# A graph network's setup: edge counts by source tile on ACT, and the fills of the message rows in the middle rounds only

## The chip, the cores and the metric

The kernel runs on one core of one Trainium2 chip. The metric is the device time of one execution in microseconds (us). It is given as the median of several runs; beside them stands one execution under the hardware profiler, from which all rows below come. The engines are PE (matrix products), DVE (vector), ACT (activations), POOL (general, and it issues the indirect DMAs) and SP (issues direct DMAs).

## The reference

Four layers of a graph network over 6250 nodes of 128 features and 100000 edges, sorted by destination. Each layer gathers rows of the nodes by `src`, weighs or transforms them, and sums them by `dst`:

```
edge_index = jnp.stack([src, dst])
h = relu(layernorm(x));  x = x + L0(h, edge_index, edge_weight, ...)
h = relu(layernorm(x));  x = x + L1(h, edge_index, ...)            # attention, two layers
h = relu(layernorm(x));  x = x + L2(h, edge_index, edge_attr_64)   # messages through an MLP
h = relu(layernorm(x));  x = x + L3(h, edge_index, ...)            # attention, 8 heads
# in L0: the message of an edge is h[col] * fsum, with fsum from tanh and cos of its edge_weight;
# row = edge_index[0] = src, col = edge_index[1] = dst, and it is summed by row
```

## The kernel before

Nodes lie in 49 tiles of 128 rows (`NB2` = 50 with one to make it even). Edges lie as 128 partitions x 784 columns (`EP`, `EC`). The kernel has a setup and then six stages, each closed by `stage_of_work` (L99 to L106): the stage's semaphores are cleared and all engines meet.

The setup sorts edges into slots: 832 tiles of 128 slots (`NT`, `SLOTS`), in which each tile holds edges of one node tile. There is one such order by destination (q = 0) and one by source (q = 1). `key[q]` holds each edge's node tile number. The setup goes so:

- **Counts** (`count_round`, L588 to L599, DVE). For each of 50 tiles and each q one instruction compares all 784 columns with the tile's number and sums the hits into `count[q]`. `looped` runs it in 25 rounds of two tiles. The compare's elementwise result goes to `equal`, scratch that shares its memory with `slots`. Then `counts_ready` is set; PE turns the counts into offsets (L468 to L471).
- **Small work** (L601 to L613): `slots` is cleared, the filter's scale and bias are made, and `filt_ready` is set. ACT's filter loop begins there (L512 to L521, Tanh, with PE's products at L462), ending in a Sin (L523).
- **Chunk 0** of the slot search (`slot_round`, DVE with help of POOL, L424 to L428), then L691 to L697, which need the filter loop, then `slot_rows`, which sets `chunk_ready`. Six more chunks follow on DVE alone.
- **Scatter** (L434 to L449, POOL). 28 rounds (`scatter_rounds` = EC / (2 * SC), SC = 14) of two halves h; each half is 14 indirect DMAs (one a column) that write 128 edge records to `rec_d`, 782 in all. Before a half, SP loads its edge attributes (L366, or L362 and L363) once the scatters of the same half one round before have landed (`scattered[h]`), and ACT copies the rest of the record (L545, L547). POOL waits for both. Ahead of them, it waits for `filled`: SP's DMA at L341 that writes empty records to the whole of `rec_d`. The last thing that POOL does in the setup is to wait for all scatters.
- **Fills of message rows** (`pad_messages`, SP, L349 to L352). Layer 0 later scatters its messages to `msg_d`, and its unused rows must hold an empty message. `msg_d` has 104 units (`NT // G`). `part` = 104 // 28 = 3 and `left` = 20. `body(i)` writes `part` units ahead of round i for i from 1 to 27; behind the rounds come units 0 to 2 and the 20 left over. SP then waits for all (`msgs_padded`).
- DVE ends its setup with the first layer norm (L199, L211), while the scatters run.

Behind the setup comes the destination pass of layer 0 (`layer0_dst_pass`, block at L1127, its scatters at L1279, first DMA L1147, DVE's first L1192), and the layers after it. SP's queue carries direct DMAs in the order written; POOL's indirect DMAs have a queue of their own.

Of the kernel before, what the change touches and what calls it, by code (L numbers as in the profile page):

```python
# [21 lines left out]
ALU = mybir.AluOpType  # L22
# [16 lines left out]
EP, EC = 128, 784  # L39
# [52 lines left out]
def gnn(nc, a, out):  # L92
# [3 lines left out]
    def sem(name):  # L96
        names[0] += 1
        return nc.alloc_semaphore(name=f"{name}_{names[0]}")
# [22 lines left out]
    with ctx:  # L121
# [92 lines left out]
        def setup():  # L214
# [33 lines left out]
            eqs, cums = [tb([EP, 2, CH], BF16) for h in range(2)], [tb([EP, 2, CH]) for h in range(2)]  # L248
            wt, cosine = tb([EP, EC]), tb([EP, EC])
            th = [tb([EP, EC]) for h in range(2)]  # L250
            diag = [tb([P, P]) for h in range(2)]
            tri, ones = tb([P, P]), tb([P, P])
            iota_t = tb([64, NTP])
# [24 lines left out]
            with stage_of_work():  # L278
# [10 lines left out]
                def spilled(v):  # L289
# [4 lines left out]
                    sem("steps_v"), sem("steps_p"))  # L294
                loop_a, loop_b, loop_c, counts_ready, offs_in_psum = (
                    sem(n) for n in ("loop_a", "loop_b", "loop_c", "counts_ready", "offs_in_psum"))
                filt_ready, cos_ready, upto_ready, upto_turned, reached_ready, tiles_counted = (
                    sem(n) for n in ("filt_ready", "cos_ready", "upto_ready", "upto_turned", "reached_ready", "tiles_counted"))
                tanh_ready, tanh_used = ([sem(f"{n}{h}") for h in range(2)] for n in ("tanh_ready", "tanh_used"))
# [5 lines left out]
                with nc.Block() as block:  # L305
                    @block.sync
                    def _(sp):
                        for q, v in enumerate(("dst", "src")):
                            sp.dma_start(node[q][:, 0:WHOLE], by_edge(a[v])).then_inc(nodes_in, 16)
                        sp.dma_start(wt[:, 0:WHOLE], by_edge(a["edge_weight"])).then_inc(edges_in, 16)  # L310
                        sp.wait_ge(spill_set, 3)
                        for q, v in enumerate(("dst", "src")):
                            sp.dma_start(node[q][0:SPILL, WHOLE:WHOLE + 1], spilled(a[v])).then_inc(nodes_in, 16)
                        sp.dma_start(wt[0:SPILL, WHOLE:WHOLE + 1], spilled(a["edge_weight"])).then_inc(edges_in, 16)
                        sp.dma_start(wf1, a["L0_gnn_Wf1"].to_broadcast([P, NF])).then_inc(edges_in, 16)
                        sp.dma_start(bf1, a["L0_gnn_bf1"].unsqueeze(0).to_broadcast([P, NF])).then_inc(edges_in, 16)
                        sp.dma_start(bf2, a["L0_gnn_bf2"].unsqueeze(0).to_broadcast([P, NF])).then_inc(edges_in, 16)
                        sp.dma_start(wf2, a["L0_gnn_Wf2"].unsqueeze(0).to_broadcast([P, NF, NF])).then_inc(edges_in, 16)
                        for t, v in vec.values():
                            sp.dma_start(t[:, :], v.unsqueeze(0).to_broadcast([P, D])).then_inc(weights_in, 16)  # L320
                        for l, t in enumerate(bias_row):
                            sp.dma_start(t[:, 0:D], a["L1_gnn_bias"][l, :].unsqueeze(0).to_broadcast([P, D])) \
                                .then_inc(weights_in, 16)
                        for t, v in mat.values():
                            sp.dma_start(t[:, :], v).then_inc(weights_in, 16)
                        for l in range(3):
                            sp.dma_start(wx[l][:, 0:D], a["L1_gnn_W"][l] if l < 2 else a["L3_gnn_W"]).then_inc(weights_in, 16)
                            for q, v in enumerate(("att_src", "att_dst")):
                                v = a["L1_gnn_" + v][l, :] if l < 2 else a["L3_gnn_" + v].rearrange("h c -> (h c)")
                                sp.dma_start(att_col[l][q][:, :], v.rearrange("(p a) -> p a", a=1)).then_inc(weights_in, 16)  # L330
                        for t, v in ((bi1_col, a["L0_gnn_bi1"]), (bu1_col, a["L2_gnn_bu1"]), (gs_col, a["L2_gnn_global_state"])):
                            sp.dma_start(t[:, :], v.rearrange("(p a) -> p a", a=1)).then_inc(weights_in, 16)
                        for t, v in ((wm1, "L2_gnn_Wm1"), (wm2, "L2_gnn_Wm2"), (wu1, "L2_gnn_Wu1"), (wu2, "L2_gnn_Wu2")):
                            sp.dma_start(t[:, :], a[v]).then_inc(weights_in, 16)

                        sp.wait_ge(x_zero, 1)
                        sp.dma_start(X[:, 0:FULL, :], a["x"][0:FULL * P, :].rearrange("(b p) f -> p b f", p=P)).then_inc(x_in, 16)
                        sp.dma_start(X[0:REST, FULL, :], a["x"][FULL * P:N, :]).then_inc(x_in, 16)

                        sp.wait_ge(pads, 1)  # L340
                        sp.dma_start(rec_d.rearrange("(k p j) w -> p k (j w)", p=P, j=G),  # L341
                                     pad_rec[:, :].unsqueeze(1).to_broadcast([P, NT // G, G * RW])).then_inc(filled, 16)


                        msg_v = msg_d.rearrange("(k p j) w -> p k (j w)", p=P, j=G)
                        scatter_rounds = EC // (2 * SC)
                        part = NT // G // scatter_rounds
                        left = NT // G - part * scatter_rounds

                        def pad_messages(k, n):  # L350
                            sp.dma_start(msg_v[:, bass.ds(k, n), :],
                                         pad_msg.unsqueeze(1).to_broadcast([P, n, G * MW])).then_inc(msgs_padded, 16)  # L352

                        def body(i, first):
                            if not first:
                                pad_messages(i * part, part)
                            for h in range(2):
                                if not first:
                                    sp.wait_ge(scattered[h], i * (16 * SC))
                                if h and isinstance(i, int) and i:  # L360
                                    at = WHOLE - (EC - SC)
                                    sp.dma_start(rec[h][:, 0:at, 0:EA], attr_v[:, EC - SC:WHOLE, :]).then_inc(attr_in[h], 16)  # L362
                                    sp.dma_start(rec[h][0:SPILL, at, 0:EA],  # L363
                                                 a["edge_attr_64"][EP * WHOLE:E]).then_inc(attr_in[h], 16)
                                else:
                                    sp.dma_start(rec[h][:, :, 0:EA],  # L366
                                                 attr_v[:, bass.ds((2 * i + h) * SC, SC), :]).then_inc(attr_in[h], 16)
                        body(0, True)
                        with sp.Fori(1, scatter_rounds - 1) as i:
                            body(i, False)  # L370
                        body(scatter_rounds - 1, False)
                        pad_messages(0, part)
                        if left:
                            pad_messages(scatter_rounds * part, left)
                        sp.wait_ge(msgs_padded, 16 * (scatter_rounds + (1 if left else 0)))

                    @block.gpsimd
                    def _(pool):
# [129 lines left out]
                    @block.scalar  # L508
                    def _(act):
                        st = Steps(act, steps_a)  # L510
                        act.wait_ge(filt_ready, 1)
                        def body(i, first):  # L512
                            for h in range(2):
# [56 lines left out]
                    def _(dve):  # L570
# [10 lines left out]
                        for q in range(2):  # L581
                            st.then(v.tensor_single_scalar(row[q][:, :], node[q][:, :], 7, ALU.logical_shift_right))
                            st.then(v.tensor_copy(key[q][:, :], row[q][:, :]))
                            st.then(v.tensor_single_scalar(row[q][:, :], node[q][:, :], P - 1, ALU.bitwise_and))
                            st.then(v.tensor_copy(meta[:, :, 4 * q:4 * q + 1], row[q][:, :].unsqueeze(2)))
                        st.then(v.tensor_copy(meta[:, :, 1:2], node[1].unsqueeze(2)))


                        def count_round(i, first):
                            for h in range(2):  # L590
                                for q in range(2):
                                    if not first:

                                        dve.wait_ge(loop_a, i * 4 + 2 * h + q - 3)
                                    b = i * 2 + h
                                    v.tensor_scalar(equal[2 * h + q], key[q], iota_row[0:EP, bass.ds(b, 1)], 0.0,
                                                    ALU.is_equal, ALU.add, accum_out=count[q][:, bass.ds(b, 1)]).then_inc(loop_a, 1)
                        looped(dve, NB2 // 2, count_round)
                        dve.wait_ge(loop_a, NB2 * 2)  # L599
                        dve.sem_inc(counts_ready, 1)  # L600
                        st.then(v.memset(slots, 0.0))  # L601
                        st.then(v.memset(slots[:, 0, WHOLE + 1:EC], float(SKIP)))
# [1307 lines left out]
```

## Time and profile before

| | us |
|---|---|
| median of 3 runs | 7402.07 (7401.49 to 7413.68) |
| the profiled execution, its own time | 7404.54 |
| its span, first to last instruction | 7402.5 |
| setup, within the span | 0 to 1304.1 |

Over the span PE is busy 3331.8 us (45%), DVE 3299.0 (45%), ACT 1691.6 (23%), POOL 5000.4 (68%). These shares are means over stages with different limits, so the prediction goes by stretches of the setup. In a row, a start is in us from the span's start, and L596 is line 596 of the kernel. A tile name such as XI, Y, H or ACC is the memory in which the setup has carved its scratch, not what the layers keep there.

### The profile page before, as it was taken

The page shows a single profiled execution, that of the slowest core. Times are in us where ns is not written, and L with a number is a line of the kernel's source. Part 1 is how long each engine was busy: PE and PEld are TensorE (multiplying, and loading weights), DVE is VectorE, ACT ScalarE, POOL GpSimd, SP SyncE. Part 2 cuts the span into 40 slices and gives each one's busy share as a digit, 9 for nine tenths or more (in the row PEclk, how much of TensorE's full clock was granted, in tenths as well). Part 3 has the DMA queues.
Part 4 walks back from the last instruction along what each step waited for, and adds up shares of the span by engine and source line. Part 5 has one row for each costly group of instructions (what it writes and reads, how often), then busy time and mean ns, then how long its engine had stood idle before and what let it go on. Part 6 is the DMA issues. An engine that isn't in the chain of part 4 may idle for free. (4 is left out here: it accounts for less than half of the span.)

```text
span 7402.5 us, 89274 instructions
## 1 busy us (share of the span) xinstructions
PE 3331.8 (45%) x17325; PEld 2957.3 (40%) x17326; DVE 3299.0 (45%) x10231; ACT 1691.6 (23%) x4176; POOL 5000.4 (68%) x5176
## 2 busy tenths in 40 slices
PE   2200000444443864444434444445777775444443
PEld 1100000444443753444434444434777664344443
DVE  8777732333323663333344333335333336544445
ACT  2200000211111963222223222223222224000000
POOL 1677777677777726777755777764777770777775
PEclk9655555666666986555556555566666677666666
DMA  6122234444443624444434444433444440444443
GB/s 225 57 92 91 96 97 151 153 156 156 155 154 133 218 79 136 129 134 131 133 91 129 133 133 130 133 100 107 134 135 134 134 128 30 132 132 133 132 132 105
DMA packets 507505, 942.53 MB, mean 127 GB/s; under 512 B 204347, under 2 KB 240683, under 8 KB 507304
## 3 DMA queue, kind: packets, MB, share of 16 engines
q1 hardware_dynamic: 349288, 637.41, 25.9%
q0 software_dynamic: 158144, 304.31, 15.8%
q8 instruction: 26, 0.43, 0.0%
q14 instruction: 47, 0.39, 0.0%
HBM read 673.90 MB, written 270.84 MB: 128 GB/s over the span
## 5 line engine op out<-in xcount | busy, mean ns | idle before, releaser
L1371 POOL DMA_INDIRECT edge_buf<-node_table,ixr x1664 | 1571.6, 944 | 619.4 <-issue 507.9
L1371 POOL DMA_INDIRECT Y<-node_table,ixr x1664 | 1569.7, 943 | 521.1 <-issue 519.9
L1111 DVE TENSOR_TENSOR ACC<-ACC,bank 128x129 f32 (+2 forms) x3744 | 1092.9, 292 | 1102.2 <-PE bank L1098 469.2
L1279 POOL DMA_INDIRECT layer_messages<-edge_buf,ixr x832 | 809.3, 973 | 295.7 <-issue 263.0
L1538 PE MATMUL bank<-adc,turned_buf 128*128 x2496 | 340.3, 195 | 1476.1 <-issue 571.7
L440 POOL DMA_INDIRECT edge_records<-edge_buf x782 | 791.2, 1012 | 255.1 <-issue 246.2
L1538 PEld LDWEIGHTS bank<-adc,turned_buf 128*128 128x128 bf16 x2496 | 257.0, 103 | 1606.7 <-issue 1552.4
L1098 PE MATMUL bank<-edge_buf,Y 128*128 128x129 f32 (+2 forms) x3744 | 821.1, 406 | 142.7 <-ACT edge_buf L1524 96.5
L1098 PE MATMUL bank<-Y 128*128 128x129 f32 (+1 forms) x3328 | 763.1, 420 | 158.6 <-ACT Y L1524 88.7
L1098 PEld LDWEIGHTS bank<-edge_buf,Y 128*128 128x128 f32 x3744 | 764.0, 309 | 173.1 <-DVE ACC L1111 136.7
L1098 PEld LDWEIGHTS bank<-Y 128*128 128x128 f32 x3328 | 713.4, 323 | 181.5 <-issue 89.0
L1486 DVE TENSOR_REDUCE pk<-bank 128x16 f32<-128x48 f32 (+1 forms) x312 | 100.5, 322 | 999.6 <-DMA Y<-node_table,ixr 501.3
L1227 PE MATMUL bank<-ident,Y 128*128 128x128 f32 x832 | 204.3, 427 | 738.7 <-DVE Y L1064 736.5
L1227 PEld LDWEIGHTS bank<-ident,Y 128*128 128x128 f32 x832 | 163.2, 223 | 761.5 <-issue 568.1
L1657 PE MATMUL bank<-wmbT,turned_buf 64*128 64x128 f32 x1664 | 293.0, 345 | 192.3 <-DVE Y L1596 101.3
L1657 PEld LDWEIGHTS bank<-wmbT,turned_buf 64*128 64x128 f32 x1664 | 266.7, 248 | 224.6 <-issue 210.1
L489 PE MATMUL bank<-Y,H 128*128 128x2 f32 (+1 forms) x6 | 1.4, 359 | 775.2 <-DVEq L717 775.2
L1239 PE MATMUL bank<-H,Y 128*128 x1664 | 318.9, 373 | 2.5 <-DVEq L1189 2.5
L1239 PEld LDWEIGHTS bank<-H,Y 128*128 128x128 f32 x1664 | 318.5, 293 | 2.8 <-issue 2.8
L1267 ACT COPY Y<-bank 128x512 f32<-128x512 f32 x208 | 123.8, 595 | 840.3 <-PE bank L1239 840.1
L1177 DVE COPY edge_buf<-XI 128x8 f32 (+1 forms) x104 | 18.7, 180 | 664.6 <-DMA layer_messages<-edge_buf,ixr 664.6
L489 PEld LDWEIGHTS bank<-Y,H 128*128 128x128 f32 x6 | 1.4, 326 | 775.4 <-issue 775.4
(279 smaller groups left out, 5319.1 us busy)
## 6 DMA issues: line engine op xcount, KB each, us to landing
Y<-onehots SPq DMA_DIRECT2D x416, 512.0 KB, 3.6
turned_buf<-onehots_turned SPq DMA_DIRECT2D x312, 256.0 KB, 3.8
edge_buf<-edge_records SPq DMA_DIRECT2D x208, 288.0 KB, 2.9
onehots<-Y SPq DMA_DIRECT2D x104, 512.0 KB, 2.7
layer_messages<-ACC SPq DMA_DIRECT2D x28, 1584.0 KB
XI<-layer_messages SPq DMA_DIRECT2D x78, 528.0 KB, 3.7
edge_records<-H SPq DMA_DIRECT2D x1, 29952.0 KB
onehots_turned<-turned_buf SPq DMA_DIRECT2D x104, 256.0 KB
```

Of the source, the lines that this page charges most:

```text
L440: pool.indirect_dma_start(rec_d, bass.IndirectOffsetOnAxis(ap=ixs[h][:, j:j + 1], axis=0), rec[h][:, j, :], None, bounds_check=SLOTS - 1, ...
L1098: ins = nc.tensor.matmul(places.at(q, j, w), tiles_of_half(onehots)[:, j, :], messages[:, j, 0:w], start=True, stop=True)
L1111: nc.vector.tensor_tensor(acc, acc, places.at(q, j, w), ALU.add).then_inc(added, 1)
L1177: nc.vector.tensor_copy(rows[h][:, :, D:D + 1], fields[:, bass.ds(t, G), R_SLOC - EA:R_SLOC - EA + 1]) \
L1227: ins = nc.tensor.transpose(bank[j // 4][:, (j % 4) * P:(j % 4) * P + P], tiles_of_half(oh[h])[:, j, :], ident[:, :])
L1239: ins = nc.tensor.matmul(bank[2 + j // 4][:, (j % 4) * P:(j % 4) * P + P], ohT[h][:, j * P:j * P + P], Hflat[:, bass.ds(at[j] * AW, D)], s ...
L1267: nc.scalar.copy(ohT[h][:, at], bank[n][:, :]).then_inc(ohT_ready, 1)
L1279: pool.indirect_dma_start(msg_d, bass.IndirectOffsetOnAxis(ap=ixr[h][:, j:j + 1], axis=0), rows[h][:, j, 0:MW], None, bounds_check=SLOTS - ...
L1371: pool.indirect_dma_start(ring[q][:, j, 0:w], None, table, bass.IndirectOffsetOnAxis(ap=ixr[q][:, j:j + 1], axis=0)).then_inc(rows_in[q], 16)
L1486: st.then(nc.vector.tensor_reduce(ps, picks(q).rearrange("p (j t k) -> p j k t", j=G, t=3), AX.X, ALU.add))
L1538: ins = nc.tensor.matmul(picks(q)[:, j * 6 * heads:(j + 1) * 6 * heads], ohbT[q][:, j * P:j * P + P], adc[:, bass.ds(at[j] * (6 * heads), ...
L1657: ins = nc.tensor.matmul(bank[2 + j // 4][:, (j % 4) * P:(j % 4) * P + P], attrT[q % 2][:, j * P:j * P + P], wmbT[:, :], start=True, stop= ...
```

## The change

ACT gets a loop of 50 Sign activations ahead of its filter loop: sign(b + 0.5 - key) over the source keys, summed along the columns into `signs[b + 1]`. The sum is (edges with key at most b) less (edges with a greater key), so the difference of neighbouring sums is twice the count of tile b. DVE counts by destination only, then waits for all the signs, subtracts and halves. SP's fills are 26 of 4 units, ahead of rounds 1 to 26, and none behind the rounds.

```diff
+            sign_at, signs = tb([EP, NB2]), tb([EP, NB2 + 1])
@@ SP
-                        part = NT // G // scatter_rounds
-                        left = NT // G - part * scatter_rounds
+                        part = -(-(NT // G) // (scatter_rounds - 2))
+                        assert part * (scatter_rounds - 2) == NT // G
...
                         def body(i, first):
-                            if not first:
-                                pad_messages(i * part, part)
+                            if not isinstance(i, int):
+                                pad_messages(i * part - part, part)
...
                         body(scatter_rounds - 1, False)
-                        pad_messages(0, part)
-                        if left:
-                            pad_messages(scatter_rounds * part, left)
-                        sp.wait_ge(msgs_padded, 16 * (scatter_rounds + (1 if left else 0)))
+                        sp.wait_ge(msgs_padded, 16 * (scatter_rounds - 2))
@@ ACT
                         st = Steps(act, steps_a)
+                        act.wait_ge(src_keys, 1)
+
+                        def sign_round(i, first):
+                            for h in range(2):
+                                b = i * 2 + h
+                                if not first:
+                                    act.wait_ge(sign_sums, i * 2 + h - 1)
+                                nc.scalar.activation(equal[2 * h + 1], key[1], ACT.Sign, scale=-1.0,
+                                                     bias=sign_at[:, bass.ds(b, 1)],
+                                                     accum_out=signs[:, bass.ds(b + 1, 1)]).then_inc(sign_sums, 1)
+                        looped(act, NB2 // 2, sign_round)
                         act.wait_ge(filt_ready, 1)
@@ DVE
                             st.then(v.tensor_copy(meta[:, :, 4 * q:4 * q + 1], row[q][:, :].unsqueeze(2)))
+                            if q:
+                                st.then(v.tensor_scalar(sign_at, iota_row[0:EP, 0:NB2], 0.5, None, ALU.add))
+                                st.then(v.memset(signs[:, 0:1], -float(EC)))
+                                dve.sem_inc(src_keys, 1)
                         st.then(v.tensor_copy(meta[:, :, 1:2], node[1].unsqueeze(2)))
...
                         def count_round(i, first):
                             for h in range(2):
-                                for q in range(2):
-                                    if not first:
-
-                                        dve.wait_ge(loop_a, i * 4 + 2 * h + q - 3)
-                                    b = i * 2 + h
-                                    v.tensor_scalar(equal[2 * h + q], key[q], iota_row[0:EP, bass.ds(b, 1)], 0.0,
-                                                    ALU.is_equal, ALU.add, accum_out=count[q][:, bass.ds(b, 1)]).then_inc(loop_a, 1)
+                                if not first:
+
+                                    dve.wait_ge(loop_a, i * 2 + h - 1)
+                                b = i * 2 + h
+                                v.tensor_scalar(equal[2 * h], key[0], iota_row[0:EP, bass.ds(b, 1)], 0.0,
+                                                ALU.is_equal, ALU.add, accum_out=count[0][:, bass.ds(b, 1)]).then_inc(loop_a, 1)
                         looped(dve, NB2 // 2, count_round)
-                        dve.wait_ge(loop_a, NB2 * 2)
+                        dve.wait_ge(loop_a, NB2)
+
+
+                        dve.wait_ge(sign_sums, NB2)
+                        st.then(v.tensor_tensor(count[1], signs[:, 1:NB2 + 1], signs[:, 0:NB2], ALU.subtract))
+                        st.then(v.tensor_scalar(count[1], count[1], 0.5, None, ALU.mult))
                         dve.sem_inc(counts_ready, 1)
```

## Rows read from the trace of the kernel before

**Rows 1.** Windows view: stretch, length, busy us of PE, PEld, DVE, ACT, POOL, clock, DMA share, GB/s.

```profile
250.50:1288.20 1037.70, 8.84 (x20) 3.10 (x20) 622.30 (x2014) 21.43 (x114) 791.20 (x782) 0.50 0.31 102
1304.10:7402.50 6098.40, 3220.57 (x17030) 2906.55 (x17030) 2459.11 (x7659) 1577.59 (x3915) 4150.80 (x4267) 0.66 0.43 130
```

**Rows 2.** Groups of instructions on DVE, setup: busy us, mean ns, idle before.

```profile
L596 DVE TENSOR_SCALAR_CACHE_REDUCE XI<-Y,iota_row 128x784 bf16<-128x784 bf16 x100 | 95.1, 1024 | 0.0
```

**Rows 3.** Timeline, counts and the work behind: start, us, engine, line, [idle before].

```profile
19.81 6.29 DVE L585 CAST ACC<-ACC 128x784 f32<-128x784 int32 x1
...
27.04 1.03 DVE L596 TENSOR_SCALAR_CACHE_REDUCE XI<-Y,iota_row 128x784 bf16<-128x784 bf16 x1
...
122.05 0.08 DVE L596 DVE_READ_ACCUMULATOR XI<-Y,iota_row  x1
...
122.64 1.36 DVE L601 MEMSET XI<- 128x1568 f32 x1 [0.51 <-DVE XI L596]
```

**Rows 4.** ACT in the setup: timeline at the filter loop, and a short copy.

```profile
130.39 0.40 ACT L517 ACTIVATE XI<-ident,H 128x128 f32<-128x128 f32 x1 [128.30 <-DVEq L614]
...
130.69 1.03 ACT L519 ACTIVATE XI<-XI,H 128x784 f32<-128x784 f32 x1
...
131.63 0.39 ACT L517 ACTIVATE XI<-ident,H 128x128 f32<-128x128 f32 x1
...
231.72 1.28 ACT L523 ACT_TABLE_LOAD   x1
...
233.01 0.95 ACT L523 ACTIVATE XI<-XI,Y 128x784 f32<-128x784 f32 x1
...
249.25 0.20 ACT L547 COPY edge_buf<-ACC 128x14 int32<-128x14 int32 x1
```

**Rows 5.** Timeline, end of chunk 0, first scatter.

```profile
241.96 0.57 DVE L691 TENSOR_SCALAR XI<-XI 128x784 f32<-128x784 f32 x1 [0.40 <-POOL XI L428]
...
250.52 1.30 POOL L440 DMA_INDIRECT edge_records<-edge_buf  x1 [8.59 <-issue]
```

**Rows 6.** The scatters: landing times (from the line's own view), and timeline beside a fill.

```profile
DMA to landing us min/median/max: 2.2/2.2/6.8
...
1221.29 0.59 SPq L351 DMA_DIRECT2D layer_messages<-ACC  x1
1222.13 0.97 POOL L440 DMA_INDIRECT edge_records<-edge_buf  x1 [0.30 <-issue]
...
1287.22 0.97 POOL L440 DMA_INDIRECT edge_records<-edge_buf  x1 [0.30 <-issue]
```

**Rows 7.** The closing: timeline, then SP's queue waits (us in total, times, longest).

```profile
1257.43 0.95 SPq L351 DMA_DIRECT2D layer_messages<-ACC  x2
...
1304.10 0.84 SPq L1147 DMA_DIRECT2D edge_buf<-edge_records  x2
...
SPq L305 <- DMA layer_messages<-ACC: 36.5, 1, 36.5
```

**Rows 8.** Block ends by line (duration ns, start us), and the pass compared with.

```profile
L305 POOLq DRAIN  x1: 9054/9054/9054, 1294.1 to 1294.1; - x1
...
L1127 POOLq DRAIN  x1: 3985/3985/3985, 2394.5 to 2394.5; - x1
...
2392.16 0.97 POOL L1279 DMA_INDIRECT layer_messages<-edge_buf,ixr  x1 [0.30 <-issue]
```

**Rows 9.** Timeline of SP's queue behind the fill of the record table.

```profile
39.46 79.09 SPq L366 DMA_DIRECT2D edge_buf<-in_edge_attr_dram  x2
```

**Rows 10.** Scatters' time to landing from 1285 to 1305, and windows of the closing.

```profile
edge_records<-edge_buf POOLq DMA_INDIRECT x3, 6.7
...
1265.00:1270.00 5.00, 0.00 (x0) 0.00 (x0) 0.00 (x0) 0.00 (x0) 3.78 (x5) 0.50 1.02 380
```

**Rows 11.** PE's filter products, and windows at their end.

```profile
L462 PE MATMUL bank<-XI 128*128 128x392 f32 x256 | 99.1, 525 | 10.0 <-ACT XI L519 8.8
...
230.00:235.00 5.00, 4.19 (x17) 2.29 (x16) 4.39 (x15) 4.45 (x8) 1.72 (x4) 1.00 0.00 0
```

More of the change, by code:

```diff
@@ L296, in setup @@
                     sem(n) for n in ("loop_a", "loop_b", "loop_c", "counts_ready", "offs_in_psum"))
+                src_keys, sign_sums = sem("src_keys"), sem("sign_sums")
                 filt_ready, cos_ready, upto_ready, upto_turned, reached_ready, tiles_counted = (
```

## The prediction

> **What bounds the kernel now.** I read the windows view first, cut at the setup's own events [rows 1]. The span is 7402.5 us. The setup takes the first 1304.1 us of it, and the change touches only that. The layers behind it (6098.4 us) keep their code, so whatever the setup loses or gains moves them as a block.
>
> Next I read the timeline of the setup, to see which engine holds it at each moment.
>
> First DVE counts. It runs 100 compare-and-sum instructions [rows 2], the first at 27.04 us; the last one's sum is read at 122.05 [rows 3]. They fill 95.1 us, so they start 0.95 us apart. Nobody else works: ACT is idle for 128.3 us until DVE has set the filter's inputs [rows 4], and PE has no counts to work on.
>
> Then comes chunk 0 of the slot search on DVE, which ends with L691 at 241.96 and the rows behind it; POOL issues its first record scatter at 250.52 [rows 5].
>
> From there POOL is the bound: 782 scatters in 1037.7 us, 1.33 us each [rows 1, 6]. DVE is busy for 622.3 us of them and ACT for 21.4, so neither sets that pace. The last scatter is issued at 1287.22 [rows 6].
>
> Last comes the end of the setup, 16.9 us from that scatter to the next stage's first DMA at 1304.10 [rows 7]. SP waits 36.5 us there for the last fills of the message rows, 3 and 20 units, which it issued only at 1257.43 [rows 7]. That wait is over at 1294.9 (1257.43 + 0.95 + 36.5), and is not what is late: POOL, behind its own wait for the scatters, spends 9.05 us in a DRAIN from 1294.1 to 1303.2 [rows 8]. All engines leave the block behind it.
>
> So three stretches in series matter: the counts, the scatters, the closing.
>
> **Part 1, the counts.** DVE loses 50 of 100 counting instructions, 50 x 0.95 = 47.5 us. It gains four small ones: before its loop an add on 128x50 and a memset (about 0.2 + 0.1 us), behind it a subtract and a multiply on 128x50 (about 0.25 us each with its wait: an estimate between the 0.08 of the sum's read [rows 3] and the 0.57 of 784 columns in L691 [rows 5]). DVE's own loop would then run from 27.35 to 27.35 + 47.5 + 0.1 = 74.95.
>
> ACT gets 50 Sign activations on 128x784 with a sum. No such operation stands in the trace, so I bound it. The same size with two pointer operands (Tanh) takes 1.03 us, with one (Sin, as Sign has) 0.95 [rows 4]. They overlap: a Tanh starts at 130.69 and the instruction behind it at 131.63 [rows 4], 0.94 us apart, so 0.09 is hidden. A Sign alone would step by 0.95 - 0.09 = 0.86 us. Its sum must be read, as DVE does in a record of its own (0.08 us [rows 3]); a short copy on ACT takes 0.20 whole [rows 4], 0.11 with the same overlap. I take the middle, 0.16, for the read: 1.02 us a Sign. ACT starts when src_keys is set, at about 26.5 (behind L585's cast at 26.10, before L586), so it ends at 26.5 + 50 x 1.02 = 77.5; with DVE's two small instructions and the signal, counts_ready falls at 78.1 in place of 122.1. **Part 1 gives 44.0 us.** Bounds: if the read costs nothing, DVE is last, 75.5, gain 46.6; if nothing overlaps (0.95 + 0.20 = 1.15 us), 84.6, gain 37.5. The value taken is nearest to the Tanh row (0.94 apart), which is the same engine, size and kind of loop.
>
> The waits added: ACT waits for the sign before the last one, which is always done when the last one starts; DVE waits for all 50 signs before it clears the slots that hold ACT's scratch output. Behind that wait stand DVE's whole setup, PE's count products and ACT's own filter loop; so it is the point where the two engines meet, and ACT is 2.5 us the later one. A second table load, should Sign need another set than Tanh, is 1.28 us [rows 4] and falls into the 8.3 us between the end of the counts and ACT's first filter step (122.05 to 130.39 [rows 3, 4]): nothing.
>
> The Trainium skill ("ScalarE: Activation LUTs", What ACT_TABLE_LOAD costs) prices an ACTIVATE with one pointer at 280 ns + 0.833 ns an element, 933 ns here, and says that neighbours overlap by 93 ns. By that a Sign steps by an estimated 0.84 us and DVE, not ACT, would be last unless the read costs over 0.13 us; the trace's 0.95 us agrees within 2%. The page gives no price for the read of the sum.
>
> Does the whole rest move up by 44 us? What else could hold POOL's first scatter: the fill of the record table lands by about 118, since SP's next issue is stuck behind it for 79.09 us from 39.46 [rows 9]. POOL would want it at about 206, so 88 us of cover are left; without the cover that fill would set the start. The first attribute loads sit behind the same fill. The filter loop (ACT and PE, until 233.96) ends 8.0 us before DVE's L691 asks for it at 241.96 [rows 4, 5], and moves by the same amount. From there all is paced by POOL's issue.
>
> **Part 2, the fills of the message rows.** Before: 27 fills of 3 units beside the rounds, and two at the end, 3 and 20 units. After: 26 of 4 units in rounds 1 to 26, none at the end. A unit is 528 KB (128 partitions x 8 x 132 words). In the rounds this adds a third to each fill, 2.1 MB. At the 380 GB/s of the closing [rows 10] that is 5.6 us in a round of two halves of 14 x (0.97 + 0.30) = 17.8 us, issued ahead of SP's wait for the scatters. The attribute load issued behind it goes out a half later. The scatters don't slow: with a fill issued at 1221.29 the next starts at 1222.13, and its 0.97 us are those of 1287.22 [rows 6]. So nothing is charged, with 12 us of cover in each half.
>
> At the end, the last scatters landed in 6.7 us beside the fills, where 2.2 is the median [rows 10, 6]. POOL's DRAIN began 6.9 us behind the last issue. A block whose POOL also ends in scatters but with idle DMA engines is the destination pass: last scatter 2392.16, DRAIN 3.985 us from 2394.5 to 2398.5 [rows 8], so 6.3 us from last issue to the end. With the 0.9 us from the DRAIN's end to the next stage, the setup would close 7.2 us behind its last scatter in place of 16.9. **Part 2 gives 9.7 us.** Bounds: if the DRAIN keeps its 9.05 us and only the landing gets shorter, 1287.2 + 2.3 + 9.05 + 0.9 = 1299.5, gain 4.6; if there were none at all, 1290.4, gain 13.7. I take the destination pass, which is the same kind of work.
>
> The Trainium skill ("DMA: Bandwidth & Descriptors", Queues, rings and completion order) says that an engine goes round robin between the queues that have work, a whole packet at a time; by that a scatter beside a fill waits for fill packets on each engine, which is what 6.7 against 2.2 us shows. It says nothing of the DRAIN.
>
> **Sum.** 44.0 + 9.7 = 53.7 us off the profiled span, 7402.5, giving 7348.8. The profiled execution's own time is 7404.5, 2.0 above its span, and the median of the runs is 7402.07, 2.5 below it; I take the gain off the median: **7348.4 us.** With the bounds of both parts the gain runs from 42.1 to 60.3, so 7341.8 to 7360.
>
> **Rivals.**
> (a) *The DRAIN stays.* SP's fills had all landed at 1294.9 and it still ran for 8.3 us more, so it may be a cost of this block; against it, the destination pass, with 832 scatters by its code, has 3.985. Gain 44.0 + 4.6: 7353.5.
> (b) *The sum makes ACT serial.* If each Sign must leave the engine and be read before the next is dispatched, and each hand-over costs what DVE idles between its last count and L601, 0.51 us [rows 3], a Sign takes 0.95 + 0.20 + 0.51 = 1.66 us: 26.5 + 83 + 0.6 = 110.1, gain 12.0 + 9.7: 7380.4. For it: no ACT sum is in the trace; against it: DVE does the same with no gap.
> (c) *Simple work is slow on ACT.* The whole gain is gone once the signs end at 131.2, a step of 2.09 us. At three times DVE's 0.95 us a Sign takes 2.85: 26.5 + 142.5 + 0.6 = 169.6, 47.5 us later than 122.1, less 9.7: 7440, slower. The Trainium skill ("ScalarE: Activation LUTs", Rules for kernel authors) advises VectorE for such operations, up to about 3 times faster in bf16. By that rule this rival would hold; the trace speaks against it, 0.94 us on ACT beside 0.95 on DVE.
> (d) *The filter loop falls to the low clock.* PE's 256 matmuls there are busy 99.1 us at a granted clock of 1.00 (2.4 GHz) [rows 11]. DVE gives them 110 us. At 0.50 (1.2 GHz) they would take 198, 88 more than that: 7348 + 88 = 7436, slower than before. It eats the whole gain once the mean clock in the loop is under 99.1 / (110 + 53.7) = 0.61. Against it: PE was idle before this loop too, longer than it will be, and had 1.00 until 235 [rows 11]; the 0.50 stands in the stretch where PE is busy for 8.84 us of 1037.7 [rows 1].
> (e) *The earlier counts don't reach POOL*, because a transfer or another engine holds the first scatter; only part 2 is left, 7392, within 0.2%. The 88 us of cover speak against it.
>
> **Chances.** Forecast 0.69, (a) 0.20, (b) 0.06, (c) 0.01, (d) 0.02, (e) 0.02. A measurement of this kernel tells 0.2% (15 us) from no change. Faster by more: forecast, (a) and (b), 0.95; same 0.02; slower 0.03. The range takes in the bounds of both parts and (a), and a few us of spread between runs: 7341 to 7362; (b) to (e), 0.11, stay outside.
>
> **What would show it.** Right: 50 Sign activations on ACT about 1.0 us apart ending near 77.5 while DVE counts until 75; the first scatter near 206.5; 782 scatters in 1038 us as before; the last one near 1243; no fill behind the rounds; POOL's closing DRAIN near 4 us; next stage at 1250.4. Wrong: Sign steps over 1.15 us; a DRAIN still near 9 us; a scatter pace over 1.33 us because of the larger fills; a stretch from counts to first scatter longer than 128.4 us.

## The result, and the profile after

The changed kernel takes 7349.3 us (median, 7346.76 to 7352.97); the kernel before took 7401.78 beside it (7401.48 to 7413.68). The ratio is 0.9928, with a 95% interval of 0.9915 to 0.9942: 52.5 us faster, where 53.7 had been forecast. The sum came so close in part by luck: two of its terms are off in opposite directions.

| stretch of the setup, us | before | forecast | after |
|---|---|---|---|
| to the first record scatter | 250.52 | 206.5 | 203.76 |
| first to last scatter issued | 1036.7 | 1036.7 | 1036.16 |
| last scatter to next stage | 16.9 | 7.2 | 12.47 |
| setup | 1304.1 | 1250.4 | 1252.39 |
| span less setup | 6098.4 | 6098.4 | 6095.1 |

In the rows, a q behind an engine's name is the engine's own instruction queue. First the groups on ACT and DVE of the changed kernel, in the setup (busy us, mean ns, idle before):

```profile
L517 ACT ACTIVATE XI<-Y 128x784 bf16<-128x784 bf16 x50 | 46.6, 932 | 24.3 <-DVEq L599 24.3
L517 ACT ACTIVATION_READ_ACCUMULATOR XI<-Y x48 | 8.9, 185 | 0.0
...
L517 ACT ACT_TABLE_LOAD x1 | 1.3, 1283 | 0.8 <-PEq L1916 0.8
L533 ACT ACT_TABLE_LOAD x1 | 1.3, 1283 | 0.0
...
L609 DVE TENSOR_SCALAR_CACHE_REDUCE XI<-Y,iota_row 128x784 bf16<-128x784 bf16 x50 | 47.6, 1026 | 0.0
```

[rows 2] had 100 counts on DVE; now it has 50, at the same pace. The timeline of the two loops' start and end:

```profile
26.34 0.95 ACT L517 ACTIVATE XI<-Y 128x784 bf16<-128x784 bf16 x1 [24.26 <-DVEq L599]
...
27.20 0.19 ACT L517 ACTIVATION_READ_ACCUMULATOR XI<-Y 128x1 f32 x1
27.29 0.93 ACT L517 ACTIVATE XI<-Y 128x784 bf16<-128x784 bf16 x1
27.32 1.03 DVE L609 TENSOR_SCALAR_CACHE_REDUCE XI<-Y,iota_row 128x784 bf16<-128x784 bf16 x1
...
72.83 0.18 ACT L517 ACTIVATION_READ_ACCUMULATOR XI<-Y  x1
...
74.82 0.08 DVE L609 DVE_READ_ACCUMULATOR XI<-Y,iota_row  x1
74.94 0.21 DVE L616 TENSOR_TENSOR XI<-XI 128x50 f32<-128x50 f32 x1
75.19 0.19 DVE L617 TENSOR_SCALAR XI<-XI 128x50 f32<-128x50 f32 x1
...
75.58 0.64 PE L468 MATMUL bank<-XI 128*128 128x50 f32 x2 [75.58 <-DVEq L618]
```

ACT is done at 73.01 and DVE at 74.90. So ACT is the early one, and DVE never waits: its subtraction follows its own last count. In [rows 3] the last sum was read at 122.05, 47.2 us later. PE's count products, which begin at 75.58, began at 122.34 before.

The groups above have two table loads, one ahead of the first Sign and one ahead of the Sin. So none stands between the Signs and the Tanhs. The timeline of the filter loop's end, as in [rows 4]:

```profile
184.42 1.28 ACT L533 ACT_TABLE_LOAD   x1
185.72 0.95 ACT L533 ACTIVATE XI<-XI,Y 128x784 f32<-128x784 f32 x1
```

The timeline of the scatters (first and last), which answers to [rows 5, 6], and of the next stage's first DMA, which answers to [rows 7]:

```profile
203.76 1.30 POOL L439 DMA_INDIRECT edge_records<-edge_buf  x1 [8.59 <-issue]
...
1239.92 0.97 POOL L439 DMA_INDIRECT edge_records<-edge_buf  x1 [0.30 <-issue]
...
1252.39 1.14 SPq L1165 DMA_DIRECT2D edge_buf<-edge_records  x2
```

And the end of the setup's block by line (duration in ns, start in us), which answers to [rows 8]. Each engine's part of a block ends with a DRAIN:

```profile
L307 SPq COMPARE_BRANCH  x1: 38/38/38, 1210.1 to 1210.1; - x1
L307 POOLq COMPARE_BRANCH  x1: 38/38/38, 1242.2 to 1242.2; - x1
L307 POOLq DRAIN  x1: 9054/9054/9054, 1242.3 to 1242.3; - x1
```

SP leaves at 1210.1, long before it is needed; POOL passes its wait 2.3 us behind the last scatter, where it had been 6.7. But the DRAIN lasts 9.054 us, as before, where 3.985 had been forecast. That is the forecast's miss.

The two profiled spans differ by 55.0 us (7402.5 and 7347.5), of which 51.7 lie in the setup and 3.3 in the layers, whose code the change leaves alone. Over the twelve profiled kernels of this case that ran at the pace of the one before, span less setup lies between 6093.5 and 6100.7 us, with no order in it; so I count these 3.3 us as spread, and the setup's 51.7 us as the effect. The medians, 52.5 us apart, agree with that within their spread.

### The profile page after: what moved, and what is told of

Same layout as the page of the kernel before. It is cut to its first block and busy times, and to the rows that moved or that the text cites. A ratio compares the mean times of both kernels' runs of the same rounds, so it can differ in the third digit from the quotient of the medians.

```text
span 7347.5 us, 89302 instructions
## 1 busy us (share of the span) xinstructions
PE 3339.2 (45%) x17325; PEld 2965.8 (40%) x17326; DVE 3231.2 (44%) x10135; ACT 1737.8 (24%) x4276; POOL 4999.3 (68%) x5176
```

## The experiments

All but the second start from the changed kernel. Stretches are read from each run's trace.

**The counts alone** (the changed kernel with SP's fills as before):

```diff
-                        part = -(-(NT // G) // (scatter_rounds - 2))
-                        assert part * (scatter_rounds - 2) == NT // G
+                        part = NT // G // scatter_rounds
+                        left = NT // G - part * scatter_rounds
...
+                        pad_messages(0, part)
+                        if left:
+                            pad_messages(scatter_rounds * part, left)
...
```

> The counts of the change with the fills of before (27 of 3 units beside the rounds, 3 and 20 units at the end). In the trace of the changed kernel the first scatter came 46.8 us earlier and the closing was 4.4 us shorter. Theory, the two parts add: first scatter at 203.8, the closing 16.9 us from the last scatter to the next stage as before, time 7401.8 - 46.8 = 7355. Rival, the parts meet (the wider fills slow the scatters or the earlier counts move them into the record table's fill): the scatters' stretch is not 1036 us and the time is off 7355 by more than 4.

Measured 7355.3 us beside 7402.75 (ratio 0.9938, 0.9922 to 0.9955), 47.45 less. First scatter at 204.62, scatters' stretch 1036.5, closing 16.9. With the 4.25 of the next run the parts add to 51.7 us, for 52.5 together. The first scatter comes 0.86 us later than the changed kernel's: DVE's cast ahead of the counts (L595 in the changed kernel) already starts 0.84 us later (20.45 for 19.61), so a single trace gives part 1 to some 0.9 us.

**The fills alone** (the kernel before with the changed kernel's SP code):

> The fills of the change with the counts of before. Theory (the DRAIN stays at its 9.05 us, only the landing of the last scatters gets shorter): first scatter at 250.5, closing 12.4 us in place of 16.9, time 7401.8 - 4.4 = 7397.4. Rival as in the prediction's main line (the DRAIN shrinks to 4 us without the fills beside it): closing 7.2 us, time 7392.

Measured 7398.5 us beside 7402.75 (ratio 0.9995, 0.9985 to 1.0004): too small to tell from no change by the time alone. In its trace the first scatter is at 250.25, the last at 1286.93, and the next stage starts at 1299.39: a closing of 12.5 us. Its DRAIN:

```profile
L305 POOLq DRAIN  x1: 9054/9054/9054, 1289.3 to 1289.3; - x1
```

So the second part is worth 4.4 us of closing: without fills at the end the last scatters land sooner (the DRAIN starts 2.4 us behind the last of them, 6.9 before). The larger fills cost the scatters nothing: 1036.7 us from first to last, as before.

**Each Sign twice**, which makes ACT late on purpose:

```diff
...
+                                if not first:
+                                    act.wait_ge(twice, i * 2 + h - 1)
+                                nc.scalar.activation(th[h], key[1], ACT.Sign, scale=-1.0,
+                                                     bias=sign_at[:, bass.ds(b, 1)],
+                                                     accum_out=spare[:, bass.ds(b, 1)]).then_inc(twice, 1)
                         looped(act, NB2 // 2, sign_round)
+                        act.wait_ge(twice, NB2)
```

> The changed kernel with each Sign activation run twice (the second into spare scratch and a spare sum), so ACT has 100 of them. It makes ACT the late engine on purpose. Theory, a Sign with its sum takes 0.93 us from start to start (the read of the sum is hidden but for 0.09): the signs end at 26.3 + 93.4 = 119.7, counts about 44.5 us later than in the changed kernel, and all behind moves one for one: first scatter near 248.3, time 7349 + 44.5 = 7394. Rival, there is slack behind the counts (something else holds the first scatter): less than 44.5. Rival of the prediction's price, 1.02 us a Sign: ends at 128.5, first scatter near 257.

Measured 7397.07 us (one execution). Timeline of its last signs, and its first scatter:

```profile
117.17 0.93 ACT L523 ACTIVATE XI<-Y 128x784 f32<-128x784 bf16 x1
118.00 0.18 ACT L523 ACTIVATION_READ_ACCUMULATOR XI<-Y  x1
118.10 0.93 ACT L518 ACTIVATE XI<-Y 128x784 bf16<-128x784 bf16 x1
118.94 0.19 ACT L518 ACTIVATION_READ_ACCUMULATOR XI<-Y  x1
...
119.87 0.18 ACT L523 ACTIVATION_READ_ACCUMULATOR XI<-Y  x1
...
248.06 1.30 POOL L440 DMA_INDIRECT edge_records<-edge_buf  x1 [8.59 <-issue]
```

The signs start 0.93 us apart (117.17, 118.10) also with 100 of them, and end at 120.05. The second Sign of each pair writes a sum that nobody uses; DVE waits only for the first. DVE's subtraction came at 119.23 for 74.94, 44.3 us later, and the first scatter too (248.06 for 203.76): the stretch behind the counts has no slack, which is what makes part 1 count in full.

**POOL's last wait on ACT:**

```diff
@@ POOL
-                        for h in range(2):
-                            pool.wait_ge(scattered[h], 16 * (SC * (last + 1) - (unused if h else 0)))
@@ ACT, behind its last rounds
+                        for h in range(2):
+                            act.wait_ge(scattered[h], 16 * (SC * (EC // (2 * SC)) - (EC - WHOLE - 1 if h else 0)))
```

> The changed kernel, with POOL's last wait (for the landing of all scatters) taken by ACT, so POOL's closing DRAIN is dispatched right behind its last scatter, as in the blocks that gather. Theory A, the DRAIN ends 5.3 us behind the end of the last indirect DMA (as in the gather blocks, where it starts early and lasts 20.1 us): the setup closes at about 1240.9 + 5.3 + 0.9 = 1247.1 in place of 1252.4, time 5.3 us less, 7344. Theory B, the DRAIN is a fixed 9.05 us of work behind the last scatter: 1240.9 + 9.05 + 0.9 = 1250.9, 1.5 us less. Theory C, the DRAIN's length belongs to the wait ahead of it and it grows by what the wait loses: no change.

Measured 7349.15 us, the same as the changed kernel's 7349.3. In the trace:

```profile
1240.44 0.97 POOL L439 DMA_INDIRECT edge_records<-edge_buf  x1 [0.30 <-issue]
...
1251.50 1.14 SPq L1165 DMA_DIRECT2D edge_buf<-edge_records  x2
...
L307 POOLq DRAIN  x1: 24354/24354/24354, 1226.1 to 1226.1; - x1
```

The DRAIN is dispatched some 12 scatters early and ends at 1250.45, 9.04 us behind the end of the last scatter (1241.41). That is theory B's number: some 9.05 us behind the last indirect DMA, whoever waits. The closing is 11.06 us in place of 12.47, 1.4 us that the time can't show.

**Work ahead of the DRAIN:**

```diff
+            idle_work = tb([P, 800])
...
                             pool.wait_ge(scattered[h], 16 * (SC * (last + 1) - (unused if h else 0)))
+                        for n in range(5):
+                            st.then(pool.memset(idle_work, 0.0))
```

> The changed kernel, POOL clears a spare tile of 128 x 800 five times (about 1 us each) between its last wait and the closing DRAIN. Theory A, the DRAIN's 9.05 us are work that goes on by itself once the scatters have landed, and POOL only waits for it: the DRAIN shrinks by what the clearing takes, about 5 us, and the setup closes at the same time, 12.5 us behind the last scatter. Theory B, the work starts with the DRAIN: it stays 9.05 us and the closing grows to 17.5 us.

Measured 7355.03 us (one execution). Beside this run and the next two the kernel before took 7407.80 us. The five clears and the DRAIN:

```profile
1242.15 4.05 POOL L453 MEMSET XI<- 128x800 f32 x5 [1.30 <-DMA edge_records<-edge_buf]
...
L308 POOLq DRAIN  x1: 9049/9049/9049, 1246.4 to 1246.4; - x1
```

It does not shrink by the 4.05 us: the closing grew to 16.6. Theory A is out, in that what the DRAIN waits for does not go on while POOL clears. Whether it begins with the DRAIN itself, as theory B has it, is settled by the last two runs.

**Halves of 7 columns** (`SC = 7`, 52 fills of 2 units) and **all rounds in POOL's loop** (784 scatters, none in straight code):

> The changed kernel with 56 rounds of two halves of 7 columns (SC = 7) in place of 28 of 14, and 52 fills of 2 units; 12 scatters stand in straight code behind POOL's loop in place of 26. Theory N, the closing DRAIN grows with the scatters of the code before it (1.88 us with none, 3.99 with 8 a half in the destination pass, 9.05 with 26 here, about 0.27 each): it becomes about 5.2 us, and the setup closes 3.9 us sooner. Theory K, it belongs to the kind of scatter or to the block: 9.05 stays. Beside that the scatters' stretch: 1036 us if a half of 8.9 us still covers the landing (2.2), ACT's copies (0.5) and SP's load (3.8), over 1040 if the 1 MB fills ahead of a load break that cover.

> The changed kernel with POOL's last round inside its loop: 28 rounds of two halves of 14, so 784 scatters (the two added columns hold no edge and are skipped by the bounds check), and no scatter in straight code behind the loop; SP loads the spilled edges ahead of the last attributes and waits for them. Theory N in its form of straight code: the DRAIN falls to about 2 us. In its form of scatters per half or per round (14 or 28): it stays between 6 and 10 us. Theory K: 9.05 us as before.

Measured 7353.11 us for the first (ratio 0.9926, 0.9910 to 0.9943, to the kernel before beside it) and 7358.47 for the second (one execution). Their DRAINs, in this order:

```profile
L307 POOLq DRAIN  x1: 9054/9054/9054, 1242.7 to 1242.7; - x1
```

```profile
L307 POOLq DRAIN  x1: 9217/9217/9217, 1245.8 to 1245.8; - x1
```

Theory N falls: 12 scatters in straight code, 26 or none, it stays near 9 us. The halves of 7 also show that the cover of a half holds at half its length: 1036.75 us from first to last scatter.

The 0.16 us more behind two more scatters led to another theory, that the DRAIN depends on the number of indirect DMAs in the block and starts again after some 113. **10, 15 and 24 more indirect DMAs** in POOL's idle time at the start test it; all their rows are skipped by the bounds check:

```diff
+            nowhere = tb([P, 1], I32)
...
                         pool.sem_inc(heads_in, 1)
+                        st.then(pool.memset(nowhere, 1 << 20))
+                        for n in range(15):
+                            pool.indirect_dma_start(tab_d[0], bass.IndirectOffsetOnAxis(ap=nowhere, axis=0),
+                                                    pad_msg[:, 0:D + 1], None, bounds_check=NBP * P - 1,
+                                                    oob_is_err=False).then_inc(early, 16)
+                        pool.wait_ge(early, 16 * 15)
```

> The changed kernel with 15 more indirect DMAs on POOL at the setup's start (rows that the bounds check skips), where POOL waits for the first slot round from about 26.5 to 89.6 us; the block then has 797 of them ahead of its closing DRAIN. The DRAIN was 9.054 us behind 782 scatters (in five kernels), 9.217 behind 784 and 3.985 behind the 832 of the destination pass. Theory R, it grows by 0.08 us for each indirect DMA and starts again after a fixed number of them; the three values agree when 782 - 832 and that number differ by 62 or 63 DMAs, which gives 113 to 114: 797 leaves 3 to 6, so the DRAIN falls to about 1.2 us, the setup closes 7.9 us sooner, time 7341 to 7342. Theory L, it grows with the scatters of the block without an end: 9.054 + 15 x 0.08 = 10.3 us. Theory K, it belongs to the block: 9.05 us. If the early DMAs slow DVE's counts beside them, the first scatter comes later than 203.8.

> As the run with 15, with 10 early indirect DMAs: 792 in the block. Theory R with a count that starts again every 113 DMAs: 1 is left, DRAIN about 0.8 to 1.9 us. Theory R with 113.8 (792 is then 109 past the sixth start): DRAIN 9.054 + 10 x 0.08 = 9.85 us. Theory K: 9.05.

> As the run with 15, with 24 early indirect DMAs: 806 in the block. Theory R (113 or 113.8): 10 to 15 past a start, DRAIN about 1.9 us. Theory L: 9.054 + 24 x 0.08 = 11.0 us. Theory K: 9.05 us.

Measured 7351.93 us for 15 (ratio 0.9930, 0.9916 to 0.9944, to 7402.69 for the kernel before), 7347.79 for 10 and 7350.17 for 24 (one execution each). The DRAIN with 15, and the other two have the same number:

```profile
L308 POOLq DRAIN  x1: 9049/9049/9049, 1242.5 to 1242.5; - x1
```

Theories R and L fall, as far as DMAs whose rows are all skipped can tell. DVE's last sum was read at 74.73 to 74.79 in all three (74.82 without them) and the first scatter came at 203.6, so indirect DMAs on POOL, with 15 of them from 28 to 47 us, cost DVE's counts beside them nothing.

**The sums of wf2 on POOL, with ACT's wait**, and **the changed kernel again** beside it:

```diff
@@ POOL, behind heads_in
+                        pool.wait_ge(edges_in, 16 * 6)
+                        for n in (32, 16, 8, 4, 2):
+                            st.then(pool.tensor_tensor(wf2[:, :, 0:n], wf2[:, :, 0:n], wf2[:, :, n:2 * n], ALU.add))
+                        st.then(pool.tensor_tensor(wf2_sum.unsqueeze(2), wf2[:, :, 0:1], wf2[:, :, 1:2], ALU.add))
+                        pool.sem_inc(wf2_added, 1)
@@ DVE
-                        st.then(v.tensor_reduce(wf2_sum, wf2, AX.X, ALU.add))
...
+                        dve.wait_ge(wf2_added, 1)
                         dve.sem_inc(filt_ready, 1)
```

> The changed kernel, with two more edits: the row sums of wf2 (one DVE instruction of 4.42 us between the counts and the filter loop) are made by POOL in six halving adds while it waits for the first slot round, and ACT in POOL's place waits for the last scatters, as in the run before with that edit. Theory, both stretches are in series with all else: first scatter at 203.8 - 4.4 = 199.3, closing 11.1 us, setup 5.8 us shorter, time about 7343.5. Rival, POOL's adds slow DVE's counts beside them (both work on the same memory in the changed kernel's first 75 us: DVE's cast took 6.29 us beside POOL's clear of 5.98): the counts end later than 74.9 and eat the gain.

> The changed kernel unchanged, on the chip of the run above, so that the two can be compared: 7349 by its earlier runs, first scatter at 203.8, setup closed at 1252.4; all theories say the same. It also shows how far the layers' 6095 us differ between executions of the same code.

These two ran on another chip, on which all three kernels are slower: 8974.95 us for the kernel before, 8904.95 for the changed one (ratio 0.9922, 0.9909 to 0.9936), 8914.04 for the one with the sums on POOL. The order of the first two is the same, with 70.0 us between them in place of 52.5; the kernel before has no trace there, so the other 17.5 us stay without a cause. What differs there is seen in the changed kernel's timeline of DVE in a chunk, and in what ACT waits for (us in total, times, longest):

```profile
806.15 0.45 DVE L665 TENSOR_TENSOR_SCAN XI<-Y,H 128x112 f32<-128x112 bf16 x1 [2.51 <-issue]
807.55 0.45 DVE L665 TENSOR_TENSOR_SCAN XI<-Y,H 128x112 f32<-128x112 bf16 x1 [0.95 <-issue]
...
ACT edge_buf L555 <- DVEq L698: 592.4, 6, 116.6
```

DVE's instructions take what they took (these scans 450 ns in the middle, 439 before), but 0.95 us and more pass between them with nothing to wait for. The register operations of DVE's own queue on the scans' line, 64 ns at most in the changed kernel's first trace, take up to 1395 ns here. DVE's chunks become the bound: ACT waits 592.4 us for them and the scatters' stretch is 1527.1 us. There the kernel with the sums on POOL had its last sum read at 74.73 (75.23 in the other trace), so POOL's adds did not slow the counts. DVE began its slot search 4.9 us earlier (82.71 for 87.65), but the first scatter came only 3.3 us earlier (200.99 for 204.29), where 4.4 were expected. The closing was 11.07 for 12.48, as expected. But its scatters took 3.2 us longer, so its setup ended only 1.55 us sooner (1742.32 for 1743.87), and the layers behind, of the same code, took 11.3 us more (7172.0 for 7160.7). I have no cause for these 11.3 us, and no run at the usual pace; so it isn't a version that beats the changed kernel.

The same two traces correct theory B. The closings are those of the usual pace (12.48 for 12.47 us with POOL's wait, 11.07 for 11.06 with ACT's), though the DRAIN itself is shorter. The changed kernel, then the one with the sums on POOL:

```profile
L307 POOLq COMPARE_BRANCH  x1: 700/700/700, 1733.8 to 1733.8; - x1
L307 POOLq DRAIN  x1: 7673/7673/7673, 1735.2 to 1735.2; - x1
```

```profile
1731.25 0.97 POOL L444 DMA_INDIRECT edge_records<-edge_buf  x1 [0.30 <-issue]
...
L307 POOLq DRAIN  x1: 7702/7702/7702, 1733.6 to 1733.6; - x1
```

Both DRAINs are dispatched some 1.4 us late, and both still end on time. The first ends at 1742.9, 9.1 us behind the branch that follows POOL's wait (9.1 to 9.4 at the usual pace). The second ends at 1741.30, 9.08 us behind the end of the last scatter (9.04 with ACT's wait at the usual pace). So the 9 us begin when POOL's last instruction or wait is over, and not with the DRAIN; its record shows what is left of them. Between POOL's last work and the DRAIN's end lie 9.0 to 9.4 us in all the setups traced, while the DRAIN's own record runs from 7.67 to 24.35.

## Why the prediction was right or wrong

- **DVE's loop**: forecast 27.35 to 74.95, measured 27.32 to 74.90. Right.
- **The price of a Sign**: 1.02 us was taken, 0.93 measured. The term that was mis-sized is the read of the sum. It takes 0.185 us whole, close to the 0.20 that was borrowed from a short copy, but only 0.09 of it shows in the step: the next Sign starts halfway through it (27.20, 27.29). The Sign itself adds 0.84 to the step, where 0.86 was taken. Half of the read was to be hidden by the overlap and then a middle was taken; the lower value, 0.11, would have been the better one. So ACT ends at 73.0 and not 77.5, DVE is the late engine, and part 1 gives 46.8 us by the first scatter, which is the upper bound that was worked out (46.6), and not 44.0. The rivals (b) and (c), a Sign of 1.66 or 2.85 us, are out. The Trainium skill ("ScalarE: Activation LUTs", What ACT_TABLE_LOAD costs) prices an activation of this size with one pointer operand at an estimated 933 ns and overlaps neighbours by 93 ns. The trace agrees: 932 ns for a Sign. By these figures DVE is last if the read adds under 0.13 us, and it adds 0.09.
- **The way from counts to scatters**: forecast to move whole. 128.4 us before, 128.86 after (74.90 to 203.76, with the 0.4 us of the two new DVE instructions in it). Right; with each Sign twice it moved whole in the other direction. (e) is out.
- **The filter loop's clock**: (d) is out. The loop ended at 186.67, 8.5 us before the 195.20 at which DVE asks for it (8.0 before the change). PE's 256 products were busy 95.1 us, 99.1 in [rows 11], and the granted clock of the loop was 1.00 (2.4 GHz), the last number but two of this windows row:

```profile
84.00:184.00 100.00, 93.10 (x251) 43.59 (x252) 85.33 (x283) 83.99 (x128) 37.70 (x88) 1.00 0.47 169
```

- **The larger fills**: forecast at nothing; the scatters' stretch is 1036.16 for 1036.7, and 1036.7 with the fills alone. Right.
- **The closing**: forecast 7.2 us by the destination pass's DRAIN of 3.985; measured 12.47, with 9.054. This step failed, and rival (a), priced at 4.6 us of gain, is what happened (4.4). The step's reason was that the pass is the same kind of work, with more of it. The landing did shrink from 6.7 to 2.3 us, so the half of the mechanism that rested on the fills was right. The DRAIN was not lengthened by the fills: it is 9.054 us with them at the end and without. The better reading was at hand in rival (a) itself: SP's fills had all landed 8.3 us before it ended.
- **The sum**: 2.8 us too little in part 1, 5.3 us too much in part 2, and 0.5 us less between the first and last scatter, for which nothing was forecast: 51.7 us in the setup for 53.7. That 7348.4 was forecast and 7349.3 measured is luck in part: part 2 gave less than half of its term, and part 1 covered for half of the miss.

What stays open is what sets the DRAIN. These runs show that it is not the fills (9.054 with and without), not the landing of the last scatters (with ACT's wait the 9 us begin before it), not the number of indirect DMAs (782, 792, 797, 806), nor their number in straight code (12, 26; with none, and two scatters more, it was 9.217, and the 0.16 us are unexplained). A run with another width of record, or with the same scatters in a later block, was not made.

## What to carry to other kernels

Two engines that share a loop halve it if a piece takes both about as long (0.93 and 0.95 us here), and the gain counts in full if nothing else holds what stands behind it; price the helper's instruction by its step and not its duration, and give the range both orders of who is late. When a wait at a stage's end is removed, look at what its neighbours do behind their own waits: here SP waited 36.5 us, but POOL's DRAIN ended last and did not depend on that wait; the 4.4 us came from scatters that landed sooner without the fills beside them. A term taken over from another block, as the 3.985 us were, needs a reason why the two blocks are alike. An effect of 0.06% is read from the stretch in the trace, and not from the time.

## What the runs showed of the hardware

- The read of ACT's sum is an instruction of its own, 185 ns long, half of it hidden: a Sign over 784 columns with its sum steps by 0.93 us, a compare with its sum on DVE by 0.95.
- POOL's DRAIN at the end of a block with indirect DMAs is 9.05 us in this setup, 3.98 to 3.99 in the destination pass, each within 8 ns in kernel after kernel (9.217 with all scatters in the loop). In the setup it ends 9.0 to 9.4 us behind POOL's last instruction or wait, whether it is dispatched 15 us before that or 1.4 us after; 4.05 us of clears on POOL don't shorten it.
- An indirect scatter landed 6.7 us behind its issue beside direct fills of 380 GB/s, and 2.2 in the median; the pace of issue (0.97 + 0.30 us) was the same.
- On the other chip the same program took 21% longer. In the slot search DVE's instructions kept their durations (scans 450 ns for 439), with 0.95 us and more of idle time without a releaser between them, register operations of DVE's queue on the scans' line lasted up to 1395 ns (64 before), and the branch ahead of POOL's DRAIN 700 ns (38 before).
